# Expert stage: products of full fp32 replaced by three short-fp32 products, weights streamed through six slots

## The reference, cut to what matters

```
x = x + attn0(layernorm(x)); x = x + expert(layernorm(x))
x = x + attn1(layernorm(x)); x = x + mixture(layernorm(x))

expert(h):                                    # per token, D = 256
  q = h @ Wq                                  # 2 sides x 4 heads x 64
  sim = q . keys                              # 2 x 4 x 64 similarities
  scores = best 8 of the sums of the best 8 of each side, per head
  w = silu(h . down[expert]) * softmax(scores)
  out = sum of w * up[expert]                 # 1024 experts
      + (silu(h @ Wg + bg) * (h @ Wu + bu)) @ Wd + bd      # 1024 wide
```

## Time and profile before

| | us |
|---|---|
| median of 3 runs | 4440.13 (4440.07 to 4441.22) |
| profiled execution, span from first to last instruction | 4440.5 |
| PE busy | 4192.7 (94%) |
| DVE busy | 2790.9 (63%) |
| ACT busy | 2654.5 (60%) |
| POOL busy | 1452.8 (33%) |
| mean granted PE clock | 0.978 of full speed |

### The profile page before, as it was taken

The page is one execution under the profiler, slowest core; times in us unless marked ns, Lnnn a source line. Parts: engine busy times, 40 slices in busy tenths (PEclk is TensorE's granted clock), DMA queues, the critical chain, the costliest instruction groups (busy, mean ns, idle before and its releaser), DMA issues. The chain is left out here.

```text
span 4440.5 us, 62548 instructions
## 1 busy us (share of the span) xinstructions
PE 4192.7 (94%) x22580; PEld 2203.7 (50%) x22580; DVE 2790.9 (63%) x5566; ACT 2654.5 (60%) x3193; POOL 1452.8 (33%) x1111
## 2 busy tenths in 40 slices
PE   7999999999978999999999999998899999999999
PEld 4444444544535565565565565555344444444443
DVE  6777777777748677676676645554455554555553
ACT  2555555555556454454454423444688888888888
POOL 3111111111125343343343322221354544545545
PEclk7999999999999999999999999999899999999999
DMA  7333433433210000000000001000766667667673
GB/s 176 89 94 74 102 74 81 95 96 80 60 56 1 0 1 1 1 1 1 1 1 1 1 8 26 1 1 1 166 143 161 152 143 164 149 153 162 141 162 90
DMA packets 145746, 322.79 MB, mean 73 GB/s; under 512 B 39296, under 2 KB 64272, under 8 KB 129056
## 3 DMA queue, kind: packets, MB, share of 16 engines
q1 hardware_dynamic: 137456, 310.88, 30.5%
q10 hardware_dynamic: 7920, 7.87, 0.6%
q0 software_dynamic: 64, 0.05, 0.0%
HBM read 237.93 MB, written 80.74 MB: 72 GB/s over the span
## 5 line engine op out<-in xcount | busy, mean ns | idle before, releaser
L2108 ACT ACTIVATE gelu_out<-hidden,b_col 128x1024 f32<-128x1024 f32 x1024 | 1084.4, 1112 | 164.6 <-PE hidden L2008 163.8
L648 DVE TENSOR_REDUCE maxima<-front 128x1 f32<-128x512 f32 (+3 forms) x1280 | 738.3, 631 | 170.7 <-PE front L458 97.2
L2090 POOL TENSOR_TENSOR combined<-combined,gated 128x512 f32<-128x512 f32 x480 | 619.6, 1291 | 666.9 <-DVE gated L2205 458.9
L550 ACT ACTIVATE probsT<-scoresT 128x1024 f32<-128x1024 f32 (+3 forms) x768 | 584.1, 811 | 306.1 <-PE scoresT L486 301.6
L1061 POOL TENSOR_TENSOR pair_sums<-sims 128x1024 f32<-128x1024 f32 x256 | 481.9, 1903 | 784.5 <-DVEq L1187 516.7
L2205 DVE SCALAR_TENSOR_TENSOR gated<-expert_out,b_col,gates_spread 128x512 f32<-128x512 f32 x480 | 360.1, 750 | 501.9 <-PE expert_out L2018 296.2
L2008 PE MATMUL hidden<-slice_stack,w_stack 128*128 128x512 f32 x2048 | 628.0, 428 | 15.0 <-ACT gelu_out L2108 15.0
L2018 PE MATMUL expert_out<-gelu_out,w_sb 128*32 128x512 f32 x4096 | 548.6, 608 | 24.9 <-DVE gated L2205 13.5
L2008 PEld LDWEIGHTS hidden<-slice_stack,w_stack 128*128 128x128 f32 x2048 | 352.4, 189 | 371.8 <-ACT gelu_out L2108 283.1
L399 POOL TENSOR_SCALAR_AFFINE_SELECT probsT<-probsT 128x512 f32<-128x512 f32 x256 | 163.3, 638 | 1075.4 <-ACT probsT L550 1075.4
L452 PE MATMUL front<-k_stack,q_stack 62*128 62x512 f32 (+3 forms) x1536 | 434.8, 427 | 34.6 <-DVE maxima L648 14.7
(11 more groups left out here) (203 smaller groups left out, 5663.0 us busy)
## 6 DMA issues: line engine op xcount, KB each, us to landing
gates_spread<-gate_scratch SPq DMA_DIRECT2D x512, 256.0 KB, 4.9
stack_scratch<-split_parts SPq DMA_DIRECT2D x192, 256.0 KB, 3.0
slice_stack<-slice_scratch SPq DMA_DIRECT2D x128, 256.0 KB, 8.1
q_stack<-stack_scratch SPq DMA_DIRECT2D x64, 384.0 KB, 6.2
k_stack<-stack_scratch SPq DMA_DIRECT2D x64, 384.0 KB, 9.2
slice_scratch<-slice_parts SPq DMA_DIRECT2D x32, 512.0 KB, 6.4
out_x<-x_tiles ACTq DMA_DIRECT2D x15, 512.0 KB, 4.8
x_tiles<-in_L_attn_x SPq DMA_DIRECT2D x7, 1024.0 KB, 12.3
```

Source lines behind the costliest of these rows:

```text
L550: nc.scalar.activation(PT[:, i % NPT, 2 * pr:2 * pr + 2, at:BANK], ST[pr][:, :, at:BANK], ACT.Exp, scale=SCALE).then_inc(probs_ready, 1)
L648: nc.vector.tensor_reduce(dst, F[k % 3][:, 0:parts * w].rearrange("p (a k) -> p a k", a=parts), AX.X, ALU.max)\
L2090: nc.gpsimd.tensor_tensor(CM[:, par, hc, :], CM[:, par, hc, :], Y[:, u % 2, :], ALU.add)\
L2108: nc.scalar.activation(GH[:, k % 4, :, :], HP[k % HPB][:, :, :], ACT.Gelu, bias=b1c[:, u % E:u % E + 1])\
```

## The change

Wg, Wu, the down embedding and the similarity weights are stored as a high part (rounded to short fp32) and a low part (the rest); so is x. Each product becomes three: high x high, high x low, low x high. The parts of Wg and Wu are made in 64 pieces of 128 x 64 during the causal attention: POOL loads, ACT rounds, POOL subtracts and stores to a DRAM scratch. Those of the down embedding are made in `expert_weights`: ACT rounds, DVE subtracts, SP stores. In the expert stage SP streams the 24 units of each macro, 256 KB each, from the scratch into six slots. `DT`, `wg` and `wu` are gone from SBUF. x is split from the turned bank after ACT's copy by a DVE subtraction. ACT's copies of x, DVE's last addition and the tile statistics change their places.

```
 class DenseParts:
     def load_piece(self, pool, raw, k):
         i, f, c, h = self.pieces[k]
         wait(pool, self.low_made, k)
         pool.dma_start(raw[:, :], self.weights[i][...]).then_inc(self.raw_in, 16)
     def high_part(self, act, raw, parts, k):
         act.wait_ge(self.raw_in, 16 * (k + 1))
         wait(act, self.stored, 16 * k)
         self.nc.scalar.activation(parts[:, 0, :], raw[:, :], ACT.Copy).then_inc(self.high_made, 1)
     def low_part(self, pool, raw, parts, k):
         pool.wait_ge(self.high_made, k + 1)
         self.nc.gpsimd.tensor_tensor(parts[:, 1, :], raw[:, :], parts[:, 0, :].bitcast(F32), ALU.subtract)\
             .then_inc(self.low_made, 1)
         pool.wait_ge(self.low_made, k + 1)
         pool.dma_start(self.scratch[...], parts[:, :, :].bitcast(F32)).then_inc(self.stored, 16)

 causal_attention, POOL (EVERY = 4):
-            for i in MASKED:
+            for k, i in enumerate(MASKED):
                 ...
+                if k // EVERY < len(dense.pieces) and k % EVERY == 0:
+                    dense.load_piece(pool, RAW, k // EVERY)
+                if k // EVERY < len(dense.pieces) and k % EVERY == EVERY - 1:
+                    dense.low_part(pool, RAW, PARTS, k // EVERY)
 causal_attention, ACT, after the exponential:
+                if pr == 1 and i in HIGH_AT:
+                    dense.high_part(act, RAW, PARTS, HIGH_AT[i])
 ...
+            HIGH_AT = {MASKED[EVERY * k + EVERY - 2]: k for k in range(len(dense.pieces))}

 expert_weights (down embedding; the similarity weights alike, without a store):
+                for b in range(NB):
+                    act.wait_ge(filled, NC + b + 1)
+                    ...
+                    nc.scalar.activation(DP[:, b, 0, :, :], ps[:, 0:D]..., ACT.Copy).then_inc(high, 1)
+                for b in range(NB):
+                    dve.wait_ge(high, b + 1)
+                    nc.vector.tensor_tensor(DP[:, b, 1, :, :], ps[:, 0:D]..., DP[:, b, 0, :, :]..., ALU.subtract)
+                for b in range(NB):
+                    sp.wait_ge(copied_dve, copies(NC + b))
+                    sp.dma_start(dense.scratch[b], DP[:, b, :, :, :].bitcast(F32)).then_inc(dense.down_stored, 16)

 expert_ffn:
-        MT = sb("sim_weights", [P, DC, 2 * H * NK])
-        DT = sb("downT", [P, DC, NE])
-        wg = sb("wg_sb", [P, DC, FF])
-        wu = sb("wu_sb", [P, DC, FF])
-        XT = sb("xnT0", [P, 2, DC, TM])
+        MT = sb("sim_weights", [P, 2, DC, 2 * H * NK], F32R)
+        DW = sb("dense_weights", [P, dense_w.SLOTS, 2, DC, P], F32R)
+        XT = sb("xnT0", [P, 2, 2, DC, TM], F32R)
+        PARTS = ((0, 0), (0, 1), (1, 0))
 SP:
+            for u in range(UNITS * NM):
+                if u == 0:
+                    sp.wait_ge(dense_w.down_stored, 16 * NB)
+                if u == NB:
+                    sp.wait_ge(dense_w.stored, 16 * len(dense_w.pieces))
+                if u >= SLOTS:
+                    product_done(u - SLOTS)
+                sp.dma_start(DW[:, u % SLOTS, :, :, :].bitcast(F32), dense_w.scratch[u % UNITS])\
+                  .then_inc(slot_in[u % SLOTS], 16)
 PE:
+            def dense_unit(bank, m, n):
+                u = UNITS * m + n
+                pe.wait_ge(slot_in[u % SLOTS], 16 * (u // SLOTS + 1))
+                for c in range(DC):
+                    for i, (a, b) in enumerate(PARTS):
+                        mm = nc.tensor.matmul(bank[:, :], DW[:, u % SLOTS, a, c, :], XT[:, m % 2, b, c, :],
+                                              start=(c + i == 0), stop=(c == DC - 1 and i == 2))
+                return mm
-                    for c in range(DC):
-                        mm = nc.tensor.matmul(R[e % 4][:, :], DT[:, c, e * P:(e + 1) * P], XT[:, m % 2, c, :],
-                                              start=(c == 0), stop=(c == DC - 1))
-                    mm.then_inc(dg_done, 1)
+                    dense_unit(R[e % 4], m, e).then_inc(dg_done, 1)
 consumed, and the first 16 units:
-                    pe.wait_ge(front_free, front_at(m, "xs".index(kind), t))
+                    pe.wait_ge(x_split if kind == "x" else sims_copied, TT * m + t + 1)
 ACT:
-                        exps(m + 1, t)
-                    for j, (kind, n, tile, _) in enumerate(units):
-                        if kind != "w" and j // 4 == t:
-                            copy_front(R[j % 2], n, "xs".index(kind), tile)
+                    for h in range(H) if m + 1 < NM else ():
+                        if h == H - 1:
+                            copies(m, "x", t)
+                        exp_pairs(m + 1, t, h)
+                    copies(m, "s", t)
 DVE:
+            def split(bank, m, t):
+                dve.wait_ge(x_high, TT * m + t + 1)
+                x = XT[:, m % 2, :, :, t * P:(t + 1) * P]
+                nc.vector.tensor_tensor(x[:, 1], bank[:, 0:D].rearrange("p (c t) -> p c t", c=DC), x[:, 0].bitcast(F32),
+                                        ALU.subtract).then_inc(x_split, 1)
 first_half:
+                    if f == FB - 4:
+                        stats(m - 1)
 second_half:
-                        choose(m + 1, t)
+                    for h in range(H) if more else ():
+                        choose_head(m + 1, t, h)
+                        if h == H - 2 and t < 2 and m + 2 < NM:
+                            split(R[0], m + 2, 2 * t)
+                            split(R[1], m + 2, 2 * t + 1)
+                        if h == H - 2 and t == TT - 1:
+                            add(m, t)
                 if more:
                     rest_to_last(m + 1)
-                add(m, TT - 1)
-                dve.drain()
-                for t in range(TT):
-                    tile_stats(nc, X, STATS, TT * m + t)
+                else:
+                    add(m, TT - 1)
+                    stats(m)
```

More of the change, by code:

```diff
@@ L88, in _, with __init__, load_piece, high_part @@
                 nc.scalar.activation(SD, VE, ACT.Sqrt).then_inc(sd_ready, 1)
-def causal_attention(nc, x, X, STATS, MEAN, RS, B, Wq, Wk, Wv, ident):
+class DenseParts:
+    COLS = 64
+    SLOTS = 6
+    def __init__(self, nc, ctx, Wg, Wu):
+        self.nc = nc
+        self.weights = Wg, Wu
+        self.FB = Wg.shape[1] // P
+        self.DOWN = 8
+        self.UNITS = self.DOWN + 2 * self.FB
+        self.scratch = nc.dram_tensor("dense_scratch", [self.UNITS, P, 2, DC, P], F32).ap()
+        self.pieces = [(i, f, c, h) for i in range(2) for f in range(self.FB) for c in range(DC)
+                       for h in range(P // self.COLS)]
+        self.raw_in = ctx.enter_context(nc.semaphore("dense_raw_in"))
+        self.high_made = ctx.enter_context(nc.semaphore("dense_high_made"))
+        self.low_made = ctx.enter_context(nc.semaphore("dense_low_made"))
+        self.stored = ctx.enter_context(nc.semaphore("dense_stored"))
+        self.down_stored = ctx.enter_context(nc.semaphore("down_stored"))
+    def load_piece(self, pool, raw, k):
+        i, f, c, h = self.pieces[k]
+        wait(pool, self.low_made, k)
+        pool.dma_start(raw[:, :], self.weights[i][c * P:(c + 1) * P, f * P + h * self.COLS:f * P + (h + 1) * self.COLS])\
+            .then_inc(self.raw_in, 16)
+    def high_part(self, act, raw, parts, k):
+        act.wait_ge(self.raw_in, 16 * (k + 1))
+        wait(act, self.stored, 16 * k)
+        self.nc.scalar.activation(parts[:, 0, :], raw[:, :], ACT.Copy).then_inc(self.high_made, 1)
+    def low_part(self, pool, raw, parts, k):
+        i, f, c, h = self.pieces[k]
+        pool.wait_ge(self.high_made, k + 1)
+        self.nc.gpsimd.tensor_tensor(parts[:, 1, :], raw[:, :], parts[:, 0, :].bitcast(F32), ALU.subtract)\
+            .then_inc(self.low_made, 1)
+        pool.wait_ge(self.low_made, k + 1)
+        pool.dma_start(self.scratch[self.DOWN + 2 * f + i, :, :, c, h * self.COLS:(h + 1) * self.COLS],
+                       parts[:, :, :].bitcast(F32)).then_inc(self.stored, 16)
+def causal_attention(nc, x, X, STATS, MEAN, RS, B, Wq, Wk, Wv, ident, dense):
     H, HS = Wq.shape[0], Wq.shape[2]
@@ L711, in expert_weights, with copies @@
     NP = len(PAIRS)
+    NC = 2 * NP
+    def copies(n):
+        return n // 2 + 1 if n < NC else NP + n + 1 - NC
     with ExitStack() as ctx:
@@ L763, in _ @@
                 dve.wait_ge(zeroed, 1)
-                for n in range(0, 2 * NP + NB + DC, 2):
+                for n in range(0, NC, 2):
                     dve.wait_ge(filled, n + 1)
@@ L784, in _ @@
                 act.wait_ge(zeroed, 1)
-                for n in range(1, 2 * NP + NB + DC, 2):
+                for n in range(1, NC, 2):
                     act.wait_ge(filled, n + 1)
@@ L1009, in dense @@
                         pe.wait_ge(h_done, FB * m + f - 1)
-                    for c in range(DC):
-                        mm = nc.tensor.matmul(R[2 + f % 2][:, :], wu[:, c, f * P:(f + 1) * P], XT[:, m % 2, c, :],
-                                              start=(c == 0), stop=(c == DC - 1))
```

(15 more changed lines are left out.)

119 lines of the change are left out of this document (72 added, 47 removed).

## The result

The changed kernel takes 4410.86 us, median of 4 runs (4403.25 to 4422.38); the kernel before, timed beside it, 4440.68 (4440.07 to 4442.83). The ratio is 0.9935, 95% interval 0.9918 to 0.9952. So the change gains 30 us where 70 were forecast: the right side, inside the range of 4300 to 4425, and less than half the size. The profiled execution took 4403.25 us with a span of 4401.5.

The account below looks back on a forecast made before the run. PE was taken to bound the expert stage, DVE nearly the second bound in its output part. Terms -64, -15, +3, +1 and +5 sum to -70 us, giving 4370; range 4300 to 4425, held at 0.8.

Parts of the forecast that it names:

- Products: Expert stage, dense part: six short matmuls at 0.234 us make a unit 1.404 instead of 1.716; 24 units save 7.5 us.
- Rival (a): Expert stage: short products take 0.215 us each, 51 us less, 4319, or 4296 without the clock's fall; chance 0.17.
- Rival (d): Expert stage: weight loads not pulled ahead, 0.307 us per matmul, 195 us more, 4565; chance 0.05.
- rival (e): Expert stage: each product as slow as before, 2.57 us per unit, 384 us over the time before, 4825; chance 0.01.
- Output part: Second part of a steady macro: x's splits delay the bank, similarity units return 1.25 us; 42.5 us, +0.8.
- Clock: Steady macros: slow matmuls at half clock after the new 2.7 us PE gap, 1.8 us each; bounds 0 and 3.6.
- Macros 14 and 15: Last two expert-stage macros: no next-but-one tile, so no splits, only the dense part's gain; -15 us together.
- Macro 0 and start: Expert stage's beginning: PE waits for ACT and DVE, faster products buy nothing; splits cost 4 us, moved statistics return 1.4; +3.
- Stream: Expert stage's weight loads by SP: 256 KB land in 2.8 us, needed five units (7.0 us) later; cost 0.
- rival (b): Expert stage: weight loads landing in 8.1 us bind, 52 us more, 4422; chance 0.15, in part or whole.
- Attention stage: 64 pieces made during causal attention: ACT waits some 0.5 us 26 times, plus roundings; +5 us, bounds 0 and 30.
- rival (c): Causal attention: ACT's queue stands behind POOL's load, landing in 9.2 us; 204 us, 4574; chance 0.07.

Follow-up runs that it names:

- both edits: Changed kernel with POOL instead of ACT rounding the pieces and DVE's splits of x one head earlier: 4324.72 us, ratio 0.9738 to the kernel before.
- the pieces alone: Kernel before plus only the 64 pieces' loads, roundings, subtractions and stores in the attention stage, scratch never read, expert stage old: 4505.87 us, ratio 1.0149.
- the raw pieces ahead: Changed kernel with a second raw buffer, POOL issuing each piece's load four masks earlier: 4386.7 us, ratio 0.9879 to the kernel before.

## Where the prediction was right and which step failed

**Products: right.** The forecast took 0.234 us between starts from the mixture stage; they are 0.230 apart, and the dense part is 33.2 us, where 33.7 were forecast. Over 24 units of six, 0.004 us make the half microsecond. Rival (a), 0.215, falls, and with it what the Trainium skill (TensorE: Matmul & The Clock Gate, "Back-to-back issue gap") gives as the gap of an isolated matmul of 512 columns, 216 ns: the measured spacing at full clock, 230 ns, disagrees with it for this type. Rival (d), loads not pulled ahead, and rival (e), products as slow as before, fall by the same row.

**Output part: right in mechanism, 0.4 too dear.** The gap that the splits make before tile 2's weights are turned was forecast at 2.7 us and is 2.62, ended by the split's line. The part is 42.1 us (1681.05 to 1723.12) against 42.5.

**Clock: half right.** Charged were 1.8 us for every steady macro. Macros 1 to 5 paid none, 6 to 13 paid 1.5 to 1.7 each, behind the same gap. So 23 us were charged and some 13 paid. With this the steady macros gained 5 x 7.5 + 8 x 5.95 = 85 us instead of 64. Moving the splits ahead of a head gave back 14 us, all in the expert stage. That the clock is lost in some macros only is measured; what decides between them stays open.

**Macros 14 and 15, macro 0, preparation.** Macros 14 and 15 gained 17.5, against 15 forecast. "Macro 0 and start" was forecast at +3 and came to +0.9. The start, from the stage's first turning to macro 0's first dense product, where the splits of macros 0 and 1 stand, took 20.9 us instead of 17.8, so 3.1 more. Macro 0 itself gained 2.2 (108.8 to 106.6 between dense starts): its dense part, to the first turning of the experts' weights, fell from 58.2 (1320.81 to 1378.98) to 55.4 us (1390.79 to 1446.18), and its output part rose by 0.5. The forecast gave the faster products nothing there, from one wait in the output part. The preparation lost 0.6, forecast 1.

**Stream: right.** The landing is 2.8 us, as in the nearest row in kind; rival (b), at 8.1, falls. The price of a late stream was checked with three slots.

**Attention stage: the step that failed.** The prediction said: "Transfers that POOL issued landed in 2.9 us. So ACT waits some 0.5 us 26 times", took +5 and set the upper bound at 30. It was 66, and the prediction's own sign of being wrong, an attention stage that grows by tens of us, came true. The rows behind the 2.9 were two transfers at 25 us. The median of the 64 is 2.9 indeed, but the wait is made by the tail: 16 of 64 at 6.3 us or more. A median times a count stood where a sum over the distribution should have stood, and ACT's slack of 1 to 3.6 us per piece, which could cover a median, is short of waits of up to 6.2 us. The mechanism is that of rival (c), given 0.07: ACT's queue behind POOL's load. I had priced it with 9.2 us for every piece, 204 us, and let it decide the sign at 6.3 (its 7.3 and 5.3 us of lateness are 6.7 and 4.5 if counted as the forecast counts, 9.2 less 2.5 and 4.7, which gives 172); with the true mixture it costs about a third of that and takes most of the gain without turning it. Between the forecast (2.9 always) and the rival (9.2 always) the case in which both hold had no number of its own, though the range reached it. The bound of 30 for ACT's own time also left out what PE loses behind it: 36 us of the 66 are the same matmuls at a lower clock (1163.25 against 1126.87), and 29 are idle time (1250 - 1163.25 over the stretch, against 1185 - 1126.87). From its first instruction to the start of the expert stage, the granted clock is at the lower of its two levels for 181 us in the kernel after; before, for 96; where POOL rounds, 113; with both edits, 102.

The sum, then: +66 - 102 + 1 - 4 = -39 on the profiled executions; the median of the runs gives -30, since the profiled one was the fastest of the four. That this lies in the range of 4300 to 4425 is luck. The attention stage missed by +61, which alone would have given 4431; the expert stage missed by -26 (about 11 from the clock, 8 from the products, 5 from the output part, 2 from macro 0 and the start) and hid part of it. Some -4 in the later layers is there in all versions (-2.4 to -4.3), also in the one with the pieces alone (1779.0 against 1782.5); it has no explanation here, and only one execution of the kernel before was profiled.

**What stays open.** Which landings are long can be seen in the traces; why was not tested. In the kernel after, the 16 loads that POOL issued within 3.7 us after SP's last request for a q or k stack took 6.3 to 9.7 us, and no other load took more than 5.1; the 27 issued with nothing of SP's in flight took 1.9 to 2.7. Five other versions with the pieces show the same division (16 or 17 loads of 5.9 to 10.3 us each). But no run moved the loads away from SP's, and in 14 of the 16 cases POOL's own store of the piece before was in flight too, so the stacks are the likely cause and not a shown one. Nor did a run separate ACT's direct hold on PE from the loss through the clock; both vanish together when POOL rounds.

## What to carry to other kernels

Before an in-order engine is made to wait for a transfer, lay all the landings, the slowest too and not the median, over its slack: the wait is the sum of what juts out, and whatever stands behind it in the queue pays, here with 36 us through the clock beside 29 of idle time. Preparation that is meant to hide in another stage belongs on the engine that can be late (POOL here) together with its rounding; leaving that one small instruction, and its wait, on the engine that PE's next scores depend on cost 66 us. And a part of a change that adds work elsewhere is worth a run by itself: the sum of -102 and +66 looked like a small gain.

## What the runs showed of the hardware that I had not expected

- 32 KB loads issued by POOL landed in 1.9 to 9.7 us (median 2.9) in one stage with a DMA share of 0.35, while 256 KB loads in the expert stage landed in 2.4 to 4.7 (median 2.8). Here the small loads had the longest landings, and those were the ones issued just after large ones of SP's.
- The same gap of 2.62 us is followed by full clock in macros 1 to 5 and by slow matmuls in macros 6 to 13. With POOL rounding, the slow ones are macro 1 and then 8 to 13; with the raw pieces ahead, 4 to 13. The instructions are the same in each.
- A short-fp32 matmul of 512 columns with its own weight load costs 0.230 us, against 0.429 for one of the two instructions of a full-fp32 product. Three short products cost 0.690 us a block of inputs, full fp32 0.858: a saving of a fifth.
